# Halving each weighting of a strided-attention kernel, in a new order of the step

## The chip, the cores and the metric

One core of one Trainium2 chip runs the kernel. The metric is the device time of one execution in microseconds. Engines are named as in the profile: PE (TensorE) does matmuls, DVE (VectorE) and ACT (ScalarE) read their results, POOL (GpSimd) works in SBUF only, SP issues DMAs.

## The reference

`x` is 4 x 2048 x 256. After a layer norm, the result is `x` plus attention plus a linear layer whose input is rounded to fp8. The attention has 16 heads of 16 columns, and a key is allowed for a query when its number is a multiple of 4 ("far") or at most 8 away ("near"):

```python
allowed = (j % 4 == 0) | (jnp.abs(i - j) <= 8)
scores = jnp.einsum('bhqd,bhkd->bhqk', q, k) / jnp.sqrt(D)      # D = 16
attn = softmax(jnp.where(allowed, scores, -inf))
out = jnp.einsum('bhqk,bhkd->bhqd', attn, v)                     # then @ o_w + o_b
return x + out + ffn                                             # ffn: fp8-rounded xn @ w8.T + bias
```

## The kernel before

A first part (to about 240 us) projects q, k and v, writes them to DRAM with the keys sorted by stride, and computes the linear layer into `base`. The second part, `part_attend`, is what the change touches; a last part multiplies by `o_w` and adds, from about 1137 us.

**Steps.** The attention is cut into 64 steps, `Step` (line 639): one step is 512 queries of one batch for a group of 4 heads. All engines run the same unrolled list of steps, each its own function, and meet at semaphores. In a step TensorE computes 16 far scores (`("far", r, h)`: 128 of the 512 far keys, head h, 512 queries, L1065) and 4 near scores (`("near", h)`, a mask product L1069 and four products L1071), each into one of four PSUM banks `ps_s`. ACT takes the exponential of each into `probs` (L948, L953).

**Units.** The maxima that are subtracted are found by a second set of products, with queries on the partitions: 16 far units (`far_unit(tile, h)`, L1095) and 4 near units (`near_unit(half, two)`, two mask products L1103 and four products L1109), each into one of three banks `ps_u`. DVE takes the maximum of each (L1019, L1022). These run ahead of the scores: the units of index 0 to AHEAD - 1 in the list `MAXIMA` belong to the next step, the others to the one after it. At index AHEAD DVE combines the two kinds into `peak` (L1003); POOL makes the negated fp16 parts of it (L807 to L813, `negmax`), TensorE turns them (`("negmax",)`, L1061), ACT copies them and issues two DMAs into rows of `q_op` (L932), and the next step's first score waits for those.

**Weighing.** `weigh(st, d, r)` multiplies `probs` by v, in fp32, for the four heads side by side in four groups of 32 columns of the array; all five rounds (four far, one near) add up in one bank, `ps_o`. The last column group of v holds ones, which gives the sums. A weighing waits until ACT has written the probabilities of its round. `weigh_own` is of this step, `weigh_last` of the step before. After the last one ACT copies `ps_o` to `out_rows` (L917, at `COPY_AFTER`) and moves the sums by DMA (L924). DVE takes their reciprocal at index TURN (L996), SP stores it and loads it spread over rows (L868, L889), POOL multiplies (L800), SP stores the result (L894). Between these SP loads q (L87), k (L78, L79) and v (L831) of later steps in pieces.

**Order.** TensorE's order within a step is written out in `body` of `tensor_attend`: a score, a unit, a score, a unit, and a weighing after every few of these pairs. A score uses the upper or lower half of the array's rows by its head (heads 0 and 1, heads 2 and 3), a unit likewise, and most pairs take one of each. `SCORES` gives the scores' order to the other engines, `MAXIMA` that of the units. A score waits for ACT's reading of the score four before it, a unit for DVE's reading of the unit three before it.

Of the kernel before, what the change touches and what calls it, by code (L numbers as in the profile page):

```python
# [15 lines left out]
P = 128  # L16
KC = H // P
CH = 512
# [72 lines left out]
def part_project(nc, io, dram, keep, ctx):  # L91
# [526 lines left out]
COPY_AFTER, MOVE_AFTER = ("far", 1, 1), ("far", 1, 2)  # L618
LOAD_AFTER = SCORES[SCORES.index(("negmax",)) + 1]
MAXIMA = (  # L620
    ("far", 0, 2), ("far", 0, 3), ("far", 0, 0), ("far", 0, 1), ("near", 1, 0),
    ("far", 1, 2), ("near", 0, 0), ("far", 1, 0), ("far", 1, 3), ("far", 1, 1),
    ("far", 2, 2), ("far", 2, 3), ("far", 2, 0), ("far", 2, 1), ("near", 1, 1),
    ("far", 3, 2), ("far", 3, 0), ("far", 3, 3), ("near", 0, 1), ("far", 3, 1),
)


def entries(s):
# [5 lines left out]
def part_attend(nc, io, dram, keep, out, ctx, done):  # L634
# [146 lines left out]
    def gpsimd_attend(pool):  # L781

        pool.wait_ge(done["base_ready"], B * CPB)
        heads_k = k_op[1][:].rearrange("r (h s) -> r h s", h=PAIR)
        nc.gpsimd.memset(heads_k[:, :, NS:NS + WPAD], 0.0).then_inc(pads_set, 1)
        nc.gpsimd.memset(heads_k[:, :, WPAD + S:], 0.0).then_inc(pads_set, 1)
        nc.gpsimd.memset(share_rows[:], 1.0).then_inc(pads_set, 1)

        def add_bias(c):
            rows = base[:, c].rearrange("p (t f) -> p t f", t=TT)  # L790
            nc.gpsimd.tensor_tensor(rows, rows, keep["bias"][:].unsqueeze(1).broadcast_to([P, TT, H]),
                                    ALU.add).then_inc(bias_added, 1)
# [24 lines left out]
        unrolled(body)  # L817

    def sync_attend(sp):
# [86 lines left out]
            sp.dma_start(out_tiles[B * CPB - 1, :, t], totals[:, B * CPB - 1, t]).then_inc(out_stored, 16)  # L906
        sp.wait_ge(out_stored, 16 * (B * CPB - 1 + TT))

    def scalar_attend(act):

        def copy_out(st):
# [23 lines left out]
        def body(st):  # L935
            todo = st.entries()
            for kind in todo:
                act.wait_ge(s_ready, st.entry(kind))
                if kind[0] == "negmax":
                    if st.n >= 1:  # L940
                        act.wait_ge(negmax_loaded, 16 * HALVES * st.at())
                    ins = nc.scalar.activation(negmax_rows[:, st.n % 2],
                                               ps_s[st.bank(kind)][0:PARTS * HG * TT, 0:P], ACT.Copy)
                elif kind[0] == "far":
                    r, h = kind[1:]
                    if h == 0 and st.n >= 1:
                        act.wait_ge(pv_done, ROUNDS * st.at(-1) + r + 1)
                    ins = nc.scalar.activation(probs[:, r, h], ps_s[st.bank(kind)], ACT.Exp)  # L948
                else:
                    h = kind[1]  # L950
                    if h == 0 and st.n >= 1:
                        act.wait_ge(pv_done, ROUNDS * st.at())
# [94 lines left out]
    def tensor_attend(pe):  # L1047
# [66 lines left out]
        def weigh(st, d, r):  # L1114

            v = v_op[st.parity(d)]
            if r == 0:
# [4 lines left out]
            if r < ROUNDS - 1:  # L1122
                pe.wait_ge(s_used, st.entry(("far", r, HG - 1), d))
                for h in range(HG):
                    ins = nc.tensor.matmul(ps_o[h * VW:(h + 1) * VW], v[:, r, h * VW:(h + 1) * VW], probs[:, r, h],  # L1125
                                           start=(r == 0), stop=False)
            else:
                pe.wait_ge(s_used, st.entry(("near", HG - 1), d))
                for t in range(TT):
                    tile = NS // P + st.queries(d) * TT + t  # L1130
                    for h in range(HG):
                        ins = nc.tensor.matmul(ps_o[h * VW:(h + 1) * VW, t * P:(t + 1) * P],  # L1132
                                               v[0:WIN, tile, h * VW:(h + 1) * VW],
                                               probs[0:WIN, r, h, t * P:(t + 1) * P],
                                               start=False, stop=(t == TT - 1))
            ins.then_inc(pv_done, 1)

        def body(st):
            def far_unit(tile, h):
                unit(st, ("far", tile, h))  # L1140
# [4 lines left out]
            def far(r, h):  # L1145
                if st.exists():
                    score(st, ("far", r, h))

            def near(h):
                if st.exists():  # L1150
                    score(st, ("near", h))
# [2 lines left out]
                if ("negmax",) in st.entries():  # L1154
                    score(st, ("negmax",))

            def weigh_last(r):
                if st.exists(-1):
                    weigh(st, -1, r)

            def weigh_own(r):
                if st.exists():
                    weigh(st, 0, r)

            far(0, 0)
            far_unit(0, 2)
            far(0, 1)
            far_unit(0, 3)
            weigh_last(3)
            far(0, 2)  # L1170
            far_unit(0, 0)
            far(0, 3)
            far_unit(0, 1)
            far(1, 0)
            near_unit(1, 0)
            weigh_last(4)
            far(1, 1)
            far_unit(1, 2)
            far(1, 2)
            near_unit(0, 0)  # L1180
            far(1, 3)
            far_unit(1, 0)
            near(0)
            far_unit(1, 3)
            weigh_own(0)
            near(2)
            far_unit(1, 1)
            far(2, 0)
            far_unit(2, 2)
            far(2, 1)  # L1190
            far_unit(2, 3)
            far(2, 2)
            far_unit(2, 0)
            far(2, 3)
            far_unit(2, 1)
            weigh_own(1)
            maxima()
            far(3, 0)
            near_unit(1, 1)
            far(3, 1)  # L1200
            far_unit(3, 2)
            far(3, 2)
            far_unit(3, 0)
            near(1)
            far_unit(3, 3)
            weigh_own(2)
            near(3)
            near_unit(0, 1)
            far(3, 3)
            far_unit(3, 1)  # L1210

        def project(j, n):

# [153 lines left out]
```

## Time and profile before

| | |
|---|---|
| time, median of 3 runs | 1197.07 us (1196.61 to 1198.26) |
| profiled execution, its own time | 1197.61 us |
| its span, first to last instruction | 1195.8 us |
| busy: PE, DVE, ACT, POOL | 1114.0 (93%), 996.0 (83%), 803.0 (67%), 240.8 (20%) us |
| chain that ended last | PE 73%, DVE 16%, issue 5%, POOL 3%, ACT 2% |
| dearest groups, busy us | DVE L1019 652.9; ACT L948 554.6; PE L1095 326.2; PE L1065 308.6; PE L1125 274.5 |

The busy time of PE counts each matmul from its start to its modelled end, and consecutive matmuls overlap; so the distance between starts tells more than the length of one. In a timeline a line `x2` merges two instructions that follow each other; a bracket at its end is the time that the engine sat idle before it, and what released it.

### The profile page before, as it was taken

What the parts mean: (1) busy time and instruction counts of PE and PEld (TensorE: products, weight loads), DVE (VectorE), ACT (ScalarE), POOL (GpSimd) and SP (SyncE); (2) the same over time, 40 slices, a digit from 0 to 9 for tenths busy, and PEclk for the clock granted to TensorE, in tenths of its full rate; (3) what the DMA queues carried; (4) which work ended last, traced back from release to release, by engine and by line L of the source; (5) the groups of instructions that cost most, each with busy time, mean ns of one, the idle gap of its engine ahead of it and who ended that gap; (6) DMA issues with size and microseconds to landing.
All of it is one profiled execution on the core that took longest, in us unless ns stands there. A gap on an engine that the chain in (4) does not pass through costs nothing.

```text
span 1195.8 us, 27662 instructions
## 1 busy us (share of the span) xinstructions
PE 1114.0 (93%) x10178; PEld 562.5 (47%) x10178; DVE 996.0 (83%) x1842; ACT 803.0 (67%) x1528; POOL 240.8 (20%) x318
## 2 busy tenths in 40 slices
PE   5799999999999999999999999999999999999999
PEld 3466666634444444444444444444444444444387
DVE  6778887498999999998999999999999989999333
ACT  3343344327888888888888888888888788888800
POOL 2233333301121212212121212122121212122100
PEclk9899999959999999999999999999999999999999
DMA  4566667632222323223232223222322222232278
GB/s 156 163 189 185 193 201 196 204 95 53 67 69 71 82 64 81 62 78 74 71 75 68 69 72 78 72 76 62 76 76 71 75 68 70 74 78 57 60 255 273
DMA packets 184913, 124.44 MB, mean 104 GB/s; under 512 B 50824, under 2 KB 169352, under 8 KB 184776
## 3 DMA queue, kind: packets, MB, share of 16 engines
q1 hardware_dynamic: 169888, 114.81, 34.7%
q10 hardware_dynamic: 14896, 7.93, 2.5%
q8 instruction: 78, 1.28, 0.5%
q14 instruction: 51, 0.42, 0.1%
HBM read 70.61 MB, written 50.99 MB: 102 GB/s over the span
## 4 chain that ended last, share of the span: by engine, by line
PE 73%; DVE 16%; issue 5%; POOL 3%; ACT 2%; ACTq 0%; DMA 0%; DVEq 0%; POOLq 0%
PE ps_attend L1125 21%; PE ps_attend L1095 11%; PE ps_attend L1065 8%; DVE peak_far L1019 8%; PE ps_attend L1132 5%; PE ps_attend L1069 5%; PE ps_attend L1224 4%; DVE peak_near L1022 3%; PE ps_attend L1071 3%; PE ps_attend L1109 3%; PE ps_project L563 3%; PE ps_project L573 3%; PE ps_attend L1103 3%; POOL y L288 1%; PE ps_project L588 1%
## 5 line engine op out<-in xcount | busy, mean ns | idle before, releaser
L1019 DVE TENSOR_REDUCE peak_far<-ps_attend 128x1 f32<-128x512 f32 x1024 | 652.9, 679 | 44.3 <-PE ps_attend L1095 39.5
L948 ACT ACTIVATE probs<-ps_attend 128x512 f32<-128x512 f32 x1024 | 554.6, 601 | 119.3 <-PE ps_attend L1065 58.2
L1095 PE MATMUL ps_attend<-k_op,q_op 48*128 48x512 f16 x1024 | 326.2, 389 | 49.2 <-DVE peak_far L1019 45.6
L1065 PE MATMUL ps_attend<-q_op,k_op 50*128 50x512 f16 x1024 | 308.6, 382 | 0.8 <-ACT probs L953 0.4
L1125 PE MATMUL ps_attend<-probs,v_op 128*32 128x512 f32 x2048 | 274.5, 608 | 2.8 <-ACT probs L948 2.1
L1022 DVE TENSOR_REDUCE peak_near<-ps_attend 128x4 f32<-128x432 f32 x256 | 154.0, 602 | 34.1 <-PE ps_attend L1109 34.1
L807 POOL TENSOR_SCALAR peak_rest<-peak 128x16 f32<-128x16 f32 x64 | 16.1, 252 | 704.7 <-DVE peak L1003 704.7
L1095 PEld LDWEIGHTS ps_attend<-k_op,q_op 48*128 48x128 f16 x1024 | 84.8, 94 | 140.5 <-DVE peak_far L1019 97.3
L953 ACT ACTIVATE probs<-ps_attend 108x512 f32<-108x512 f32 x256 | 144.8, 597 | 3.5 <-PE ps_attend L1071 3.3
L1065 PEld LDWEIGHTS ps_attend<-q_op,k_op 50*128 50x128 f16 x1024 | 86.2, 94 | 125.4 <-ACT probs L948 82.8
L1103 PE MATMUL ps_attend<-mask_k,mask_q 48*128 48x216 bf16 x512 | 116.7, 259 | 0.4 <-DVE peak_far L1019 0.4
L1109 PE MATMUL ps_attend<-k_op,q_op 48*128 48x108 f16 x1024 | 115.2, 209 | 0.0
L1071 PEld LDWEIGHTS ps_attend<-q_op,k_op 50*108 50x108 f16 x1024 | 93.3, 125 | 35.4 <-issue 1.1
L1069 PE MATMUL ps_attend<-mask_q,mask_k 48*108 48x512 bf16 x256 | 102.4, 400 | 0.0
L1109 PEld LDWEIGHTS ps_attend<-k_op,q_op 48*128 48x128 f16 x1024 | 96.7, 95 | 8.1
L1071 PE MATMUL ps_attend<-q_op,k_op 50*108 50x128 f16 x1024 | 99.1, 216 | 0.0
L800 POOL TENSOR_TENSOR out_rows<-out_rows,share_rows 128x512 f32<-128x512 f32 x64 | 82.0, 1281 | 31.1 <-DMA share_rows<-shares_dram 28.0
L1069 PEld LDWEIGHTS ps_attend<-mask_q,mask_k 48*108 48x108 bf16 x256 | 31.7, 124 | 109.0 <-ACT probs L948 104.8
L1125 PEld LDWEIGHTS ps_attend<-probs,v_op 128*32 128x32 f32 x2048 | 40.8, 108 | 63.0 <-issue 32.1
L1132 PE MATMUL ps_attend<-probs,v_op 108*32 108x128 f32 x2048 | 69.1, 276 | 0.0
L285 POOL TENSOR_TENSOR quant<-quant,power 128x1024 f32<-128x1024 f32 x16 | 38.5, 2404 | 125.9 <-PE ps_project L588 99.6
L537 PE MATMUL ps_project<-xnT,wq 128*128 128x512 f32 x128 | 59.3, 607 | 2.1 <-DVE wq L395 2.1
(87 smaller groups left out, 1017.2 us busy)
## 6 DMA issues: line engine op xcount, KB each, us to landing
v_dram<-v_sb SPq DMA_DIRECT2D x64, 256.0 KB, 3.0
v_op<-v_dram SPq DMA_DIRECT2D x48, 288.0 KB
q_op<-q_parts_dram SPq DMA_DIRECT2D x384, 32.0 KB, 1.9
k_op<-k_parts_dram SPq DMA_DIRECT2D x96, 96.0 KB, 2.6
base<-in_x SPq DMA_DIRECT2D x16, 512.0 KB, 4.9
q_parts_dram<-qk_parts SPq DMA_DIRECT2D x32, 256.0 KB, 3.0
share_rows<-shares_dram SPq DMA_DIRECT2D x256, 32.0 KB, 2.3
attn_dram<-out_rows SPq DMA_DIRECT2D x256, 32.0 KB, 1.7
```

The costliest lines, as they stand in the source:

```text
L948: ins = nc.scalar.activation(probs[:, r, h], ps_s[st.bank(kind)], ACT.Exp)
L953: ins = nc.scalar.activation(probs[0:WIN, ROUNDS - 1, h], ps_s[st.bank(kind)][0:WIN], ACT.Exp)
L1019: ins = nc.vector.tensor_reduce(peak_far[:, h, tile:tile + 1], bank, AX_X, ALU.max)
L1022: ins = nc.vector.tensor_reduce(peak_near[:, half * PAIR:(half + 1) * PAIR, two * 2:two * 2 + 2], near_bank(bank), AX_X, ALU.max)
L1065: ins = nc.tensor.matmul(bank, k[rows, keys(h, r * P, P)], q[rows, h % PAIR], start=True, stop=True)
L1069: nc.tensor.matmul(bank[0:WIN], mask_k[masks], mask_q[masks, at:at + CH], start=True, stop=False)
L1071: ins = nc.tensor.matmul(bank[0:WIN, t * P:(t + 1) * P], k[rows, window(h, st.queries() * TT + t)], q[rows, h % PAIR, t * P:(t + 1) * P], ...
L1095: ins = nc.tensor.matmul(bank, q[rows, h % PAIR, tile * P:(tile + 1) * P], k[rows, keys(h, 0, NS)], start=True, stop=True)
L1103: nc.tensor.matmul(near_bank(bank)[:, :, t], mask_q[masks, at + tile * P:at + (tile + 1) * P], mask_k[masks].unsqueeze(1).broadcast_to([MA ...
L1109: ins = nc.tensor.matmul(near_bank(bank)[:, r, t], q[rows, r, tile * P:(tile + 1) * P], k[rows, window(h, st.queries(d) * TT + tile)], sta ...
L1125: ins = nc.tensor.matmul(ps_o[h * VW:(h + 1) * VW], v[:, r, h * VW:(h + 1) * VW], probs[:, r, h], start=(r == 0), stop=False)
L1132: ins = nc.tensor.matmul(ps_o[h * VW:(h + 1) * VW, t * P:(t + 1) * P], v[0:WIN, tile, h * VW:(h + 1) * VW], probs[0:WIN, r, h, t * P:(t + ...
```

## The change

Each weighing is made in `SPLIT` = 2 parts. A part of a far round takes 256 of the 512 queries (columns) for the four heads; a part of the near round takes two of the four tiles. The semaphore `pv_done` counts after the second part, in the order of the new list `WEIGHINGS`: far 0, far 1, far 2, near, far 3 (`weighed` gives ACT its values). Only the first part of far 0 starts the accumulation.

The order of the step is new: after every second pair of score and unit stands one part. The four near scores and the four near units stand together, pairs 13 to 16. The last three parts of a step (near 1, far 3 0 and 1) stand behind pairs 2, 4 and 6 of the next. AHEAD goes from 10 to 4, so `peak` is made after four units of the list, and the units of tile 3 lead it; the `negmax` product follows pair 10 and not pair 14. TURN goes from 17 to 14. On POOL the multiplication of `out_rows` moves from ahead of the `negmax` chain to behind it, with its wait one step later.

```diff
-AHEAD = 10
-TURN = 17
+AHEAD = 4
+TURN = 14
 SCORES = (
     ("far", 0, 0), ("far", 0, 1), ("far", 0, 2), ("far", 0, 3), ("far", 1, 0),
-    ("far", 1, 1), ("far", 1, 2), ("far", 1, 3), ("near", 0), ("near", 2),
-    ("far", 2, 0), ("far", 2, 1), ("far", 2, 2), ("far", 2, 3), ("negmax",),
-    ("far", 3, 0), ("far", 3, 1), ("far", 3, 2), ("near", 1), ("near", 3),
+    ("far", 1, 1), ("far", 1, 2), ("far", 1, 3), ("far", 2, 0), ("far", 2, 1),
+    ("negmax",), ("far", 2, 2), ("far", 2, 3), ("near", 0), ("near", 1),
+    ("near", 2), ("near", 3), ("far", 3, 0), ("far", 3, 1), ("far", 3, 2),
     ("far", 3, 3),
 )
...
+WEIGHINGS = (("far", 0), ("far", 1), ("far", 2), ("near",), ("far", 3))
+SPLIT = 2
...
         def body(st):
-            if st.exists(-3):
-
-                rows = out_rows[:, (st.n - 3) % OUTS]
-                pool.wait_ge(negmax_ready, min(st.at(1), STEPS))
-                pool.wait_ge(shares_loaded, 16 * HG * st.at(-2))
-                nc.gpsimd.tensor_tensor(rows, rows, share_rows[:], ALU.mult).then_inc(attn_ready, 1)
             if st.exists(1):
 
-                if st.exists(-3):
-                    pool.wait_ge(attn_ready, st.at(-2))
                 pool.wait_ge(peak_ready, st.at(2))
...
+            if st.exists(-3):
+
+                rows = out_rows[:, (st.n - 3) % OUTS]
+                pool.wait_ge(negmax_ready, min(st.at(2), STEPS))
+                pool.wait_ge(shares_loaded, 16 * HG * st.at(-2))
+                nc.gpsimd.tensor_tensor(rows, rows, share_rows[:], ALU.mult).then_inc(attn_ready, 1)
...
+        def weigh(st, d, kind, part):
+
+            v, n = v_op[st.parity(d)], CH // SPLIT
+            cols = slice(part * n, (part + 1) * n)
...
                 for h in range(HG):
-                    ins = nc.tensor.matmul(ps_o[h * VW:(h + 1) * VW], v[:, r, h * VW:(h + 1) * VW], probs[:, r, h],
-                                           start=(r == 0), stop=False)
+                    ins = nc.tensor.matmul(ps_o[h * VW:(h + 1) * VW, cols], v[:, r, h * VW:(h + 1) * VW],
+                                           probs[:, r, h, cols], start=(kind == WEIGHINGS[0] and part == 0),
+                                           stop=(kind == WEIGHINGS[-1] and part == SPLIT - 1))
             else:
                 pe.wait_ge(s_used, st.entry(("near", HG - 1), d))
-                for t in range(TT):
+                for t in range(part * TT // SPLIT, (part + 1) * TT // SPLIT):
...
+            if part == SPLIT - 1:
+                ins.then_inc(pv_done, 1)
```

The order of a step after the change (it takes the place of the one in `body` above; `W` stands for `weigh_last` in the first three and `weigh_own` in the others):

```
far(0,0) far_unit(3,2)  far(0,1) far_unit(3,3)  W near 1
far(0,2) far_unit(3,0)  far(0,3) far_unit(3,1)  W far 3, 0
far(1,0) far_unit(0,2)  far(1,1) far_unit(0,3)  W far 3, 1
far(1,2) far_unit(0,0)  far(1,3) far_unit(0,1)  W far 0, 0
far(2,0) far_unit(1,2)  far(2,1) far_unit(1,3)  negmax  W far 0, 1
far(2,2) far_unit(1,0)  far(2,3) far_unit(1,1)  W far 1, 0
near(0) near_unit(1,0)  near(1) near_unit(1,1)  W far 1, 1
near(2) near_unit(0,0)  near(3) near_unit(0,1)  W far 2, 0
far(3,0) far_unit(2,2)  far(3,1) far_unit(2,3)  W far 2, 1
far(3,2) far_unit(2,0)  far(3,3) far_unit(2,1)  W near 0
```

## Rows read from the trace of the kernel before

**Rows 1.** Stretches: us; busy PE, PEld, DVE, ACT, POOL (instructions); clock; DMA; GB/s

```profile
400.00:1000.00 600.00, 565.27 (x6187) 254.73 (x6184) 545.48 (x965) 488.28 (x965) 110.78 (x187) 1.00 0.29 73
```

**Rows 2.** Timeline of VectorE, 607 to 625 us: start, length, engine, line, tiles, count, idle

```profile
607.09 0.69 DVE L1019 TENSOR_REDUCE peak_far<-ps_attend 128x1 f32<-128x512 f32 x1 [0.17 <-PE ps_attend L1095]
...
609.91 0.69 DVE L1019 TENSOR_REDUCE peak_far<-ps_attend 128x1 f32<-128x512 f32 x1 [0.42 <-PE ps_attend L1095]
...
610.84 2.48 DVE L1019 TENSOR_REDUCE peak_far<-ps_attend 128x1 f32<-128x512 f32 x4
...
615.25 0.24 DVE L996 RECIPROCAL shares<-sums 128x16 f32<-128x16 f32 x1
...
616.36 0.61 DVE L1022 TENSOR_REDUCE peak_near<-ps_attend 128x4 f32<-128x432 f32 x1 [0.32 <-PE ps_attend L1109]
616.88 3.20 DVE L1019 TENSOR_REDUCE peak_far<-ps_attend 128x1 f32<-128x512 f32 x5
...
624.51 2.48 DVE L1019 TENSOR_REDUCE peak_far<-ps_attend 128x1 f32<-128x512 f32 x4
```

**Rows 3.** Timeline of TensorE's matmuls, 603 to 617 us, same columns

```profile
603.35 0.39 PE L1095 MATMUL ps_attend<-k_op,q_op 48*128 48x512 f16 x1
603.67 1.06 PE L1125 MATMUL ps_attend<-probs,v_op 128*32 128x512 f32 x8
604.67 0.39 PE L1065 MATMUL ps_attend<-q_op,k_op 50*128 50x512 f16 x1
...
604.89 0.38 PE L1065 MATMUL ps_attend<-q_op,k_op 50*128 50x512 f16 x1
...
605.15 0.26 PE L1103 MATMUL ps_attend<-mask_k,mask_q 48*128 48x216 bf16 x1
...
605.62 1.08 PE L1132 MATMUL ps_attend<-probs,v_op 108*32 108x128 f32 x32
...
606.64 0.39 PE L1095 MATMUL ps_attend<-k_op,q_op 48*128 48x512 f16 x1
...
611.59 0.39 PE L1095 MATMUL ps_attend<-k_op,q_op 48*128 48x512 f16 x1 [0.54 <-DVE peak_far L1019]
...
615.51 0.42 PE L1069 MATMUL ps_attend<-mask_q,mask_k 48*108 48x512 bf16 x1
...
615.77 0.26 PE L1103 MATMUL ps_attend<-mask_k,mask_q 48*128 48x216 bf16 x1
...
615.99 0.38 PE L1065 MATMUL ps_attend<-q_op,k_op 50*128 50x512 f16 x1
...
616.16 0.42 PE L1095 MATMUL ps_attend<-k_op,q_op 48*128 48x512 f16 x2
```

**Rows 4.** Timeline of ACT and its DMA queue (ACTq), 613 to 616 us, same columns

```profile
613.37 1.29 ACTq L932 DMA_DIRECT2D q_op<-negmax_rows  x2
614.71 1.08 ACT L948 ACTIVATE probs<-ps_attend 128x512 f32<-128x512 f32 x2 [0.75 <-PE ps_attend L1071]
```

**Rows 5.** Groups by shape, 400 to 1000 us: count; busy us, mean ns; idle before

```profile
L1125 PE MATMUL ps_attend<-probs,v_op 128*32 128x512 f32 x1400 | 186.4, 604 | 0.8 <-ACT probs L948 0.6
...
L1132 PE MATMUL ps_attend<-probs,v_op 108*32 108x128 f32 x1408 | 47.6, 276 | 0.0
...
L1125 PEld LDWEIGHTS ps_attend<-probs,v_op 128*32 128x32 f32 x1400 | 27.9, 108 | 42.2 <-issue 22.8 <-ACT probs L948 10.7 <-ACT out_rows L917 8.7
```

**Rows 6.** DMA issues by line, 400 to 1000 us: count, KB each, median us to landing

```profile
k_op<-k_parts_dram SPq DMA_DIRECT2D x66, 96.0 KB, 2.6
```

**Rows 7.** Line 1003 (`peak`): ns min/median/max, first and last start in us

```profile
L1003 DVE TENSOR_TENSOR peak<-peak_far,peak_near x64: 174/174/176, 252.3 to 1117.1; 128x16 f32<-128x16 f32 x64
```

**Rows 8.** Timeline of VectorE, the third `peak`

```profile
282.04 0.17 DVE L1003 TENSOR_TENSOR peak<-peak_far,peak_near 128x16 f32<-128x16 f32 x1
```

**Rows 9.** The page's slices of 29.9 us each, granted TensorE clock in tenths

```profile
PEclk9899999959999999999999999999999999999999
```

**Rows 10.** Timeline of ACT, the last exponential

```profile
1134.05 0.59 ACT L948 ACTIVATE probs<-ps_attend 128x512 f32<-128x512 f32 x1
```

More of the change, by code:

```diff
@@ L620 @@
 MAXIMA = (
[L621 to L624, printed above, removed]
-)
+    ("far", 3, 2), ("far", 3, 3), ("far", 3, 0), ("far", 3, 1), ("far", 0, 2),
+    ("far", 0, 3), ("far", 0, 0), ("far", 0, 1), ("far", 1, 2), ("far", 1, 3),
+    ("far", 1, 0), ("far", 1, 1), ("near", 1, 0), ("near", 1, 1), ("near", 0, 0),
+    ("near", 0, 1), ("far", 2, 2), ("far", 2, 3), ("far", 2, 0), ("far", 2, 1),
+)
+WEIGHINGS = (("far", 0), ("far", 1), ("far", 2), ("near",), ("far", 3))
+SPLIT = 2
 def entries(s):
@@ L907, in sync_attend, with weighed @@
         sp.wait_ge(out_stored, 16 * (B * CPB - 1 + TT))
+    def weighed(st, kind):
+        return ROUNDS * st.at(-1) + WEIGHINGS.index(kind) + 1
     def scalar_attend(act):
@@ L946, in body @@
                     if h == 0 and st.n >= 1:
-                        act.wait_ge(pv_done, ROUNDS * st.at(-1) + r + 1)
+                        act.wait_ge(pv_done, weighed(st, ("far", r)))
                     ins = nc.scalar.activation(probs[:, r, h], ps_s[st.bank(kind)], ACT.Exp)
@@ L951, in body @@
                     if h == 0 and st.n >= 1:
-                        act.wait_ge(pv_done, ROUNDS * st.at())
+                        act.wait_ge(pv_done, weighed(st, ("near",)))
                     ins = nc.scalar.activation(probs[0:WIN, ROUNDS - 1, h], ps_s[st.bank(kind)][0:WIN], ACT.Exp)
@@ L1112, in unit @@
             ins.then_inc(u_ready, 1)
-        def weigh(st, d, r):
-            v = v_op[st.parity(d)]
-            if r == 0:
+        def weigh(st, d, kind, part):
+            v, n = v_op[st.parity(d)], CH // SPLIT
+            cols = slice(part * n, (part + 1) * n)
+            if kind == WEIGHINGS[0] and part == 0:
                 if st.queries(d) == 0:
@@ L1121, in weigh @@
                     pe.wait_ge(out_copied, st.at(d))
-            if r < ROUNDS - 1:
+            if kind[0] == "far":
+                r = kind[1]
                 pe.wait_ge(s_used, st.entry(("far", r, HG - 1), d))
                 for h in range(HG):
-                    ins = nc.tensor.matmul(ps_o[h * VW:(h + 1) * VW], v[:, r, h * VW:(h + 1) * VW], probs[:, r, h],
-                                           start=(r == 0), stop=False)
+                    ins = nc.tensor.matmul(ps_o[h * VW:(h + 1) * VW, cols], v[:, r, h * VW:(h + 1) * VW],
+                                           probs[:, r, h, cols], start=(kind == WEIGHINGS[0] and part == 0),
+                                           stop=(kind == WEIGHINGS[-1] and part == SPLIT - 1))
             else:
                 pe.wait_ge(s_used, st.entry(("near", HG - 1), d))
-                for t in range(TT):
+                for t in range(part * TT // SPLIT, (part + 1) * TT // SPLIT):
                     tile = NS // P + st.queries(d) * TT + t
@@ L1133, in weigh @@
                                                v[0:WIN, tile, h * VW:(h + 1) * VW],
-                                               probs[0:WIN, r, h, t * P:(t + 1) * P],
-                                               start=False, stop=(t == TT - 1))
-            ins.then_inc(pv_done, 1)
+                                               probs[0:WIN, ROUNDS - 1, h, t * P:(t + 1) * P],
+                                               start=False, stop=False)
+            if part == SPLIT - 1:
+                ins.then_inc(pv_done, 1)
         def body(st):
@@ L1155, in maxima, with weigh_last, weigh_own @@
                     score(st, ("negmax",))
-            def weigh_last(r):
+            def weigh_last(kind, part):
                 if st.exists(-1):
-                    weigh(st, -1, r)
-            def weigh_own(r):
+                    weigh(st, -1, kind, part)
+            def weigh_own(kind, part):
                 if st.exists():
-                    weigh(st, 0, r)
+                    weigh(st, 0, kind, part)
             far(0, 0)
+            far_unit(3, 2)
+            far(0, 1)
+            far_unit(3, 3)
@@ L1166, in body @@
+            weigh_last(("near",), 1)
+            far(0, 2)
+            far_unit(3, 0)
+            far(0, 3)
+            far_unit(3, 1)
+            weigh_last(("far", 3), 0)
+            far(1, 0)
             far_unit(0, 2)
-            far(0, 1)
+            far(1, 1)
             far_unit(0, 3)
-            weigh_last(3)
-            far(0, 2)
+            weigh_last(("far", 3), 1)
+            far(1, 2)
             far_unit(0, 0)
-            far(0, 3)
+            far(1, 3)
             far_unit(0, 1)
-            far(1, 0)
+            weigh_own(("far", 0), 0)
@@ L1175, in body @@
+            far(2, 0)
+            far_unit(1, 2)
+            far(2, 1)
+            far_unit(1, 3)
+            maxima()
+            weigh_own(("far", 0), 1)
+            far(2, 2)
+            far_unit(1, 0)
+            far(2, 3)
+            far_unit(1, 1)
+            weigh_own(("far", 1), 0)
+            near(0)
             near_unit(1, 0)
[L1176 to L1179, printed above, removed]
+            near(1)
+            near_unit(1, 1)
@@ L1180, in body @@
+            weigh_own(("far", 1), 1)
+            near(2)
             near_unit(0, 0)
[L1181 to L1206, printed above, removed]
             near(3)
             near_unit(0, 1)
+            weigh_own(("far", 2), 0)
+            far(3, 0)
+            far_unit(2, 2)
+            far(3, 1)
+            far_unit(2, 3)
+            weigh_own(("far", 2), 1)
+            far(3, 2)
+            far_unit(2, 0)
@@ L1209, in body @@
             far(3, 3)
-            far_unit(3, 1)
+            far_unit(2, 1)
+            weigh_own(("near",), 0)
         def project(j, n):
```

## The prediction

> **What bounds the kernel now.** I read the page's chain first: TensorE holds 73% of it and VectorE 16%, almost all in the attention part. A row of stretches gives the steady part: in 600 us TensorE's matmuls are busy 565 us and VectorE 545 us, ACT 488, at the full granted clock [rows 1]. Two engines above 90% and neither at 100% is a coupled loop; its period is read from the order of events, so the rest rests on the timeline of one step. VectorE takes 20 maxima per step (16 "far", 4 "near"). Running without a wait it starts a far maximum every 0.624 us (five in 3.20, less the last one's own 0.70, is four intervals) and the next one 0.52 us after a near one (616.36 to 616.88). The combining operation `peak` stretches one interval to 0.93 (609.91 to 610.84), 0.31 more; the reciprocal (615.25) adds 0.12 beside its neighbours [rows 2]. Without waits a step is 16 x 0.624 + 4 x 0.517 + 0.31 + 0.12 = 12.5 us; it takes 13.67 (610.84 to 624.51), and the difference is four waits, of which the first, second and last stand in the rows (607.09, 609.91, 616.36: idle 0.17, 0.42 and 0.32). Each is for a unit, the product whose maximum is taken, that TensorE made late, and before each TensorE had done a whole weighing (that before 607.09 at 605.62) [rows 2, 3]. ACT is the third engine: some 11.1 us of a step busy and about 0.8 held by its own DMA issues (idle before 614.71) [rows 1, 4].
>
> **Prices on TensorE.** A far score and a far unit use different halves of the rows and run together, 0.22 us for a pair (604.67 to 604.89). From a far unit to the weighing behind it 0.32 pass (603.35 to 603.67), 0.10 more than a pair; from the weighing to the next pair 1.00 (604.67) [rows 3]. One of its fp32 instructions of 512 columns lasts 604 ns, one of 128 columns 276 ns: 384 columns are 328 ns, 512 are 0.43 us [rows 5]. Two such passes stream 0.86, and 0.14 is the change back. So a weighing is 0.10 + 0.86 + 0.14, and the 0.24 doesn't shrink with its columns. The near weighing, in four times as many instructions of a quarter of the columns, takes 1.02 (605.62 to 606.64): more weight loads and shorter instructions cost 0.02 in all [rows 3].
>
> **Part by part.** *Halving.* Ten parts in place of five weighings. A part is 0.10 + 0.43 + 0.14 = 0.67, of which 0.565 from its start to the next pair. Five added parts are 5 x 0.24 = 1.2 us of TensorE per step; the 32 added instructions of a step's far weighings and their weight loads hide as in the near one. Bounds for an added part: not below 0.14 (the change back alone), up to 0.35, if one load of 0.108 stood open in each [rows 5]. I take 0.24.
>
> The Trainium skill (TensorEngine Tiling, Key Properties) says that changing the tiling mode, not only the tile, drains the engine. The 0.10 and the 0.14 at a weighing's two ends agree with that; the page has no price, and by its rule the change adds ten drains per step and is a loss wherever TensorE ends last.
>
> *Where the parts hide.* Three banks hold units. A bank is free 0.75 after the start of the maximum read from it (610.84 to the unit at 611.59); a unit can be read 0.45 after its start (606.64, maximum 607.09) [rows 2, 3]. In far stretches TensorE needs 0.22 + 0.32 + 0.565 = 1.11 for two pairs and a part, VectorE 1.25. Set the start of a maximum to 0: the unit into its bank starts at 0.75, the part at 1.07, the next pair at 1.63, its unit is readable at 2.08, and VectorE wants it at 2.50. So in 16 of 20 pairs there is no wait. With a whole weighing it is readable at 2.52, just late, and anything slow behind it is a wait: the four of before.
>
> *The near stretch.* The new order puts four near scores beside four near units in a row. The trace has one such pair per step: score 615.51, unit 615.77, next score 615.99, next unit 616.16, and the near unit is read at 616.36 [rows 2, 3]. So: 0.48 to the next score; the unit 0.26 behind its score after a weighing (0.22 otherwise, the score's mask product); readable 0.59 after its start; and 0.47 from a near unit to the weighing behind it (605.15 to 605.62). Walk on, 0 being the maximum of pair 9. Unit of pair 12 at 0.75 (its bank), part 1.07. Pair 13 at 1.63, readable 2.48; pair 14 at 2.11, unit 2.33, readable 2.92; part 2.80. Pair 15 at 3.37, unit 3.63, readable 4.22; pair 16 at 3.85, unit 4.07, readable 4.66; part 4.54. Pair 17, far, at 5.10, readable 5.55. VectorE: pairs 9 to 12 at 0, 0.62, 1.25, 1.87; 13 at 2.50; 14 at 3.01; 15 at 4.22 (wanted 3.53); 16 at 4.73; 17 at 5.55 (wanted 5.25). Without waits pair 17 would start at 4.57, so the near stretch costs 0.98. The reciprocal now stands before pair 15, in the first wait: its 0.12 is hidden. Pairs 19 and 21 are readable at 6.66 and 7.77, wanted at 6.80 and 8.05: no wait. **Period: 12.05 + 0.31 + 0.98 = 13.35**, 0.31 less than now. Three parts lie on this path: if a part costs d more, the period is 3d longer.
>
> *The moved steps.* `peak` comes after unit 4 and the negmax product after pair 10, six pairs (3.7 us) between them and not four: no wait. ACT's two DMA issues follow pair 11; the first score that needs a bank behind them (four ahead) has about 0.9 us in hand. The copy-out now waits for the part behind pair 6, 0.1 us on ACT, and two pairs later TensorE asks for it with some 0.3 in hand. POOL's multiplication moves behind the negmax chain of the step; SP waits for it ahead of four share loads, four stores and its last K or V pieces, so it issues them some 2 us later in the step than now, the last K piece about 11.5 us in. That lands 2.6 us later (median) [rows 6] and pair 5 of the next step asks for it, at 13.35 + 2.8: 2 us of cover, one step in four. All taken at nothing; with the K cover gone and 1 us more it would be 16 us.
>
> *Both ends.* The steps from the third `peak` to the last (282.04 to 1117.1) are 61: 61 x 0.31 = **-18.9** [rows 7, 8]. With the limit at 4, sixteen units and not ten stand alone before the first scores: first to second `peak` 20 x 0.62 + 0.2 = 12.6. TensorE's clock is at the lower of its levels, 1.2 GHz, in this part of the span (the ninth slice of 30 us at 0.5 in the granted row) [rows 9], so up to about 275 us streaming doubles: pairs 5 to 8 3.7, 9 to 12 4.0, 13 and 14 3.0, then at the upper level 1.8, 2.5, 2.5 and 0.3 for `peak`, 17.8 to the third. Together 30.4 against the 29.7 from 252.3 to 282.04: **+0.7**. At the end 36 pairs and not 30 run without units; the 30 took 1117.1 to 1134.65, the end of the last exponential, 0.59 each: **+3.5**. Behind that exponential stand two far parts, not a far and a near weighing: 1.2 and not 2.0, **-0.8** [rows 10]. Sum -15.5, from the profiled execution's own 1197.6 (span 1195.8) to 1182.1; that execution is 0.5 above the median of 1197.1, so **1181.6 us**.
>
> **Rivals.** (A) *An added part is cheaper*, or near pairs pack closer. For: some of the 0.24 may belong to the neighbours. At 0.14 it is 3 x 0.10 x 61 = 18 us less: 1163. The floor, no waits at all, is 61 x 1.2 = 73 less: near 1127. (B) *Slower: near pairs in a row don't overlap.* The one near pair of the trace is followed by a far one. If a near score waits until the near unit before it is through (616.16 and not 615.99), 0.17 comes on the path in each of the two groups: 0.34 x 61 = 21, **1202**. It decides against the change from 15.5 / 61 = 0.25 per step, 0.13 per group. Against: the score at 615.99 did start while the near unit ran. (C) *A weight load of 0.108 stands open in each part*: 3 x 0.108 x 61 = 20, 1201. Against: the near weighing. (D) *The change doesn't do what it says*, the wait only moves: ACT held by copy-out and issues, or SP's late K piece, eats the 0.25: 1197.
>
> **How the numbers follow.** Forecast (1172 to 1191) 0.50; A 0.13; B 0.13; C 0.10; D 0.14. Faster by over 0.2% (about what a measurement here can tell from no change) takes the forecast, A and a third of D: 0.68; same the larger part of the rest of D, 0.09; slower B and C: 0.23. The range reaches A's price and those of B and C: 1160 to 1204.
>
> **What would show it.** `peak` to `peak` 13.35. In VectorE's timeline two waits, before the third near maximum (0.6) and the first far one behind the near ones (0.3), none between far ones, the reciprocal free. On TensorE 0.565 from a part to the next score; 4096 instructions of 256 columns near 0.39 us each. Near score to near score 0.48 is right, 0.65 is B. A part above 0.65 to the next score is C. A unit waiting for K once in four steps, or scores waiting for ACT in each, is D. Most wrong of all would be waits between far pairs.

## The result and the profile after

The changed kernel takes 1163.5 us (median of 4 runs, 1163.0 to 1168.9) against 1196.9 us of the kernel before on the same chip: a ratio of 0.973, 95% interval 0.970 to 0.976. That is 33.4 us less. The forecast was 15.5 us less, 1181.6. The measured time lies below the 1172 to 1191 of the forecast itself and inside the whole range (1160 to 1204) only because that reaches down to the price of rival A.

The page's chain of the changed kernel, by engine:

```profile
PE 85%; DVE 6%; issue 4%; POOL 3%; ACT 1%; DVEq 0%; POOLq 0%
```

TensorE's share rises from 73% to 85%, VectorE's falls from 16% to 6%. The stretch that answers to [rows 1] (busy PE, weight loads, DVE, ACT, POOL; clock; DMA):

```profile
400.00:1000.00 600.00, 597.89 (x7929) 250.75 (x7930) 563.47 (x1006) 518.91 (x1007) 113.16 (x191) 1.00 0.30 76
```

More work fits into the same 600 us: 1006 instructions on VectorE and not 965, at the same clock. The timeline of VectorE, one step, answers to [rows 2] (L1023 and L1026 are the far and the near maxima, L1007 is `peak`):

```profile
606.47 0.18 DVE L1007 TENSOR_TENSOR peak<-peak_far,peak_near 128x16 f32<-128x16 f32 x1
606.68 4.87 DVE L1023 TENSOR_REDUCE peak_far<-ps_attend 128x1 f32<-128x512 f32 x8
611.55 1.12 DVE L1026 TENSOR_REDUCE peak_near<-ps_attend 128x4 f32<-128x432 f32 x2
612.59 0.24 DVE L1000 RECIPROCAL shares<-sums 128x16 f32<-128x16 f32 x1
613.31 1.12 DVE L1026 TENSOR_REDUCE peak_near<-ps_attend 128x4 f32<-128x432 f32 x2 [0.47 <-PE ps_attend L1113]
614.68 4.87 DVE L1023 TENSOR_REDUCE peak_far<-ps_attend 128x1 f32<-128x512 f32 x8 [0.25 <-PE ps_attend L1099]
619.58 0.17 DVE L1007 TENSOR_TENSOR peak<-peak_far,peak_near 128x16 f32<-128x16 f32 x1
```

`peak` to `peak` is 13.11 us. There are two marked waits, where the forecast had them: before the third near maximum and before the first far one behind the near ones. The eight far maxima in a row have no wait between them, and they need 4.87 us less the last one's 0.69: seven intervals of 0.60. That is the number to look at.

TensorE's matmuls in the same kernel answer to [rows 3]: two far pairs with a part behind them, then the near pairs.

```profile
603.33 0.39 PE L1099 MATMUL ps_attend<-k_op,q_op 48*128 48x512 f16 x1
603.55 0.38 PE L1069 MATMUL ps_attend<-q_op,k_op 50*128 50x512 f16 x1
603.55 0.38 PE L1099 MATMUL ps_attend<-k_op,q_op 48*128 48x512 f16 x1
603.86 0.65 PE L1139 MATMUL ps_attend<-probs,v_op 108*32 108x128 f32 x16
604.44 0.39 PE L1069 MATMUL ps_attend<-q_op,k_op 50*128 50x512 f16 x1
...
610.13 0.64 PE L1131 MATMUL ps_attend<-probs,v_op 128*32 128x256 f32 x8
610.70 0.42 PE L1073 MATMUL ps_attend<-mask_q,mask_k 48*108 48x512 bf16 x1
...
611.18 0.38 PE L1073 MATMUL ps_attend<-mask_q,mask_k 48*108 48x512 bf16 x1
```

(L1099 are the far units, L1069 the far scores, L1073 the first product of a near score, L1131 and L1139 the far and the near parts.) A part begins 0.31 after the last unit (603.55 to 603.86), and the next score 0.57 or 0.58 after the part (610.13 to 610.70, 603.86 to 604.44). Near score to near score is 0.48 (610.70 to 611.18). So every price on TensorE came out as taken, within 0.02 us.

### The profile page after: what moved, and what is told of

It is laid out like the page before. It is cut to its first block, busy times and chain, and to the rows that moved or that the text cites. A ratio compares the mean times of both kernels' runs of the same rounds, so it can differ in the third digit from the quotient of the medians.

```text
span 1161.2 us, 31698 instructions
## 1 busy us (share of the span) xinstructions
PE 1127.3 (97%) x12226; PEld 541.6 (47%) x12226; DVE 988.1 (85%) x1842; ACT 816.5 (70%) x1528; POOL 241.5 (21%) x318
## 4 chain that ended last, share of the span: by engine, by line
PE 85%; DVE 6%; issue 4%; POOL 3%; ACT 1%; DVEq 0%; POOLq 0%
PE ps_attend L1131 24%; PE ps_attend L1069 23%; PE ps_attend L1139 6%; PE ps_attend L1237 4%; PE ps_attend L1073 4%; PE ps_attend L1099 4%; PE ps_attend L1113 4%; PE ps_attend L1107 3%; PE ps_project L563 3%; PE ps_project L573 3%; PE ps_attend L1075 3%; DVE peak_far L1023 2%; POOL y L288 1%; PE ps_project L588 1%; DVE xn L446 1%
## 5 line engine op out<-in xcount | busy, mean ns | idle before, releaser
L1023 DVE TENSOR_REDUCE peak_far<-ps_attend 128x1 f32<-128x512 f32 x1024 | 623.8, 680 | 18.9 <-PE ps_attend L1099 16.5
L952 ACT ACTIVATE probs<-ps_attend 128x512 f32<-128x512 f32 x1024 | 563.9, 596 | 102.7 <-PE ps_attend L1069 30.9
L1099 PE MATMUL ps_attend<-k_op,q_op 48*128 48x512 f16 x1024 | 345.3, 392 | 5.7 <-DVE peak_far L1023 2.9
L1131 PE MATMUL ps_attend<-probs,v_op 128*32 128x256 f32 x4096 | 328.9, 392 | 0.7 <-ACT out_rows L921 0.7
L1069 PE MATMUL ps_attend<-q_op,k_op 50*128 50x512 f16 x1024 | 311.0, 384 | 0.0
L1026 DVE TENSOR_REDUCE peak_near<-ps_attend 128x4 f32<-128x432 f32 x256 | 143.7, 602 | 30.5 <-PE ps_attend L1113 30.3
L957 ACT ACTIVATE probs<-ps_attend 108x512 f32<-108x512 f32 x256 | 138.3, 595 | 14.7 <-PE ps_attend L1075 14.7
L1069 PEld LDWEIGHTS ps_attend<-q_op,k_op 50*128 50x128 f16 x1024 | 57.0, 94 | 183.1 <-ACT probs L952 142.6
L1099 PEld LDWEIGHTS ps_attend<-k_op,q_op 48*128 48x128 f16 x1024 | 90.0, 93 | 98.0 <-DVE peak_far L1023 90.4
L1131 PEld LDWEIGHTS ps_attend<-probs,v_op 128*32 128x32 f32 x4096 | 81.6, 108 | 99.5 <-issue 31.6
L1073 PE MATMUL ps_attend<-mask_q,mask_k 48*108 48x512 bf16 x256 | 101.9, 398 | 0.0
L813 POOL TENSOR_TENSOR out_rows<-out_rows,share_rows 128x512 f32<-128x512 f32 x64 | 81.7, 1277 | 35.2 <-DMA share_rows<-shares_dram 30.4
L1139 PE MATMUL ps_attend<-probs,v_op 108*32 108x128 f32 x2048 | 82.3, 279 | 0.0
L1139 PEld LDWEIGHTS ps_attend<-probs,v_op 108*32 108x32 f32 x2048 | 48.2, 109 | 39.2 <-ACT probs L952 39.2
```

The lines of the kernel that those rows point to most:

```text
L1023: ins = nc.vector.tensor_reduce(peak_far[:, h, tile:tile + 1], bank, AX_X, ALU.max)
L1026: ins = nc.vector.tensor_reduce(peak_near[:, half * PAIR:(half + 1) * PAIR, two * 2:two * 2 + 2], near_bank(bank), AX_X, ALU.max)
L1069: ins = nc.tensor.matmul(bank, k[rows, keys(h, r * P, P)], q[rows, h % PAIR], start=True, stop=True)
L1073: nc.tensor.matmul(bank[0:WIN], mask_k[masks], mask_q[masks, at:at + CH], start=True, stop=False)
L1099: ins = nc.tensor.matmul(bank, q[rows, h % PAIR, tile * P:(tile + 1) * P], k[rows, keys(h, 0, NS)], start=True, stop=True)
L1131: ins = nc.tensor.matmul(ps_o[h * VW:(h + 1) * VW, cols], v[:, r, h * VW:(h + 1) * VW], probs[:, r, h, cols], start=(kind == WEIGHINGS[0] ...
```

## The experiments

The runs ask two things: how much of the gain is the halving and how much the order, and whether the forecast missed by VectorE's pace or by the price of a part. `peak` to `peak` is the common measure: 13.66 in the kernel before (610.63 to 624.30 makes 13.67), 13.11 in the changed one.

**Whole weighings in the new order.**

```diff
-SPLIT = 2
+SPLIT = 1
...
-            weigh_last(("far", 3), 0)
...
-            weigh_last(("far", 3), 1)
+            weigh_last(("far", 3), 0)
```

(and likewise for the others: near behind pair 2, far 0 behind 10, far 1 behind 14, far 2 behind 18.)

> The changed kernel with SPLIT = 1: five whole weighings, behind pairs 2, 6, 10, 14 and 18 of the new order. Theory N (the new order brings most of the gain, the halving little): walking the step with 0.60 us per far maximum, peak to peak is 13.26 us against 13.11 of the changed kernel (one wait of 0.8 before the third near maximum, 0.1 to 0.2 behind each weighing in far stretches), so about 1173 us. Theory H (halving brings the gain, since a whole weighing is too long for three banks): back near the 13.66 of the kernel before, 1197 us.

Measured: 1175.2 us, ratio 0.982 (0.980 to 0.985), and from `peak` to `peak` in VectorE's timeline 13.32:

```profile
613.16 0.18 DVE L1007 TENSOR_TENSOR peak<-peak_far,peak_near 128x16 f32<-128x16 f32 x1
613.37 5.03 DVE L1023 TENSOR_REDUCE peak_far<-ps_attend 128x1 f32<-128x512 f32 x8
618.32 1.11 DVE L1026 TENSOR_REDUCE peak_near<-ps_attend 128x4 f32<-128x432 f32 x2
...
620.18 1.12 DVE L1026 TENSOR_REDUCE peak_near<-ps_attend 128x4 f32<-128x432 f32 x2 [0.59 <-PE ps_attend L1113]
621.22 5.22 DVE L1023 TENSOR_REDUCE peak_far<-ps_attend 128x1 f32<-128x512 f32 x8
626.48 0.17 DVE L1007 TENSOR_TENSOR peak<-peak_far,peak_near 128x16 f32<-128x16 f32 x1
```

Eight far maxima in 5.03 or 5.22 and not 4.87: the waits behind whole weighings (0.16 and 0.35) carry no bracket. The new order without the halving brings 22 of the 33 us, the halving in that order the other 12. Theory N holds. "Order" here takes in all that the change moves: AHEAD, TURN and POOL's multiplication. Only TURN was run by itself (below), so how the 22 us divide among the rest isn't shown.

**Halves in the old order.**

```diff
             far_unit(0, 3)
-            weigh_last(3)
+            weigh_last(3, 0)
             far(0, 2)
             far_unit(0, 0)
+            weigh_last(3, 1)
```

(each of the five so, the second half one pair later.)

> The kernel before, in its old order, with each weighing halved and the second half one pair later. Theory N: the halving takes away part of each wait and gives it back in five more changes of tiling on a TensorE that has little to spare: peak to peak 13.5, give or take 0.2, about 1188 us. Theory H: the halves bring the whole gain, 13.1, 1163 us.

Measured: 1200.7 us (seven executions, 1197.0 to 1205.9), ratio 1.004 (1.003 to 1.006); `peak` to `peak` 13.69 in the profiled execution, the fastest of them (609.15 to 622.84). The halving alone brings nothing. My 1188 was too low by 1%: that order puts halves beside near units in three places, and I had not walked it through. In its timeline the three marked waits of a step stand at a near maximum or at the far one right behind it (0.18 before 612.57, 0.31 before 615.44, 0.33 before 620.27). What decides between the theories, that it isn't 1163, is clear.

**Whole weighings away from the near pairs.**

```diff
-COPY_AFTER, MOVE_AFTER = ("far", 1, 1), ("far", 1, 2)
+COPY_AFTER, MOVE_AFTER = ("far", 1, 0), ("far", 1, 1)
...
-SPLIT = 2
+SPLIT = 1
```

(near behind pair 2, far 3 behind 5, far 0 behind 8, far 1 behind 11, far 2 behind 18.)

> SPLIT = 1, whole weighings behind pairs 2, 5, 8, 11 and 18, so that none stands among the four near pairs or right ahead of them; the copy-out one exponential earlier. Theory N, that what a weighing costs depends on what stands behind it: each far weighing makes VectorE wait 0.12, the near stretch nothing: peak to peak 12.67, about 1136 us. Theory H: whole weighings cost as in the kernel before, 13.6 or more, 1195 us.

Measured: 1142.1 us, ratio 0.954 (0.952 to 0.956), 21 us faster than the change with five parts fewer:

```profile
612.62 0.17 DVE L1007 TENSOR_TENSOR peak<-peak_far,peak_near 128x16 f32<-128x16 f32 x1
612.83 5.23 DVE L1023 TENSOR_REDUCE peak_far<-ps_attend 128x1 f32<-128x512 f32 x8
617.97 1.11 DVE L1026 TENSOR_REDUCE peak_near<-ps_attend 128x4 f32<-128x432 f32 x2
619.00 0.24 DVE L1000 RECIPROCAL shares<-sums 128x16 f32<-128x16 f32 x1
619.16 1.05 DVE L1026 TENSOR_REDUCE peak_near<-ps_attend 128x4 f32<-128x432 f32 x2
620.13 5.23 DVE L1023 TENSOR_REDUCE peak_far<-ps_attend 128x1 f32<-128x512 f32 x8
625.40 0.18 DVE L1007 TENSOR_TENSOR peak<-peak_far,peak_near 128x16 f32<-128x16 f32 x1
```

That is 12.78, and 12.67 was forecast. The near maxima follow each other without a wait, and this step of 20 maxima has no bracket at all, yet it is 0.67 longer than the 12.11 without waits. By the rows it is the two groups of eight, at 5.23 and not 4.87, some 0.35 each.

**The near pairs cleared, halves elsewhere.**

```diff
             weigh_own(("far", 1), 0)
+            weigh_own(("far", 1), 1)
...
-            weigh_own(("far", 1), 1)
...
-            weigh_own(("far", 2), 0)
...
+            weigh_own(("far", 2), 0)
             weigh_own(("far", 2), 1)
```

> The changed kernel with the two parts among the near pairs taken out of them: far 1 whole behind pair 12, far 2 whole behind pair 18, all else as it is. The walk gives no wait between near maxima any more, but 0.52 before the first (a whole weighing right ahead of it) and 0.2 behind pair 18: 12.11 + 0.72 = 12.85, about 1148 us. If the near pairs themselves, and not the parts among them, were what VectorE waits for, no gain: 1163.

Measured: 1143.1 us, ratio 0.955 (0.954 to 0.957), `peak` to `peak` 12.80 (610.35 to 623.15); the forecasts were 1148 us and 12.85:

```profile
610.35 0.17 DVE L1007 TENSOR_TENSOR peak<-peak_far,peak_near 128x16 f32<-128x16 f32 x1
610.55 4.87 DVE L1023 TENSOR_REDUCE peak_far<-ps_attend 128x1 f32<-128x512 f32 x8
615.86 1.12 DVE L1026 TENSOR_REDUCE peak_near<-ps_attend 128x4 f32<-128x432 f32 x2 [0.43 <-PE ps_attend L1113]
616.90 0.24 DVE L1000 RECIPROCAL shares<-sums 128x16 f32<-128x16 f32 x1
617.06 1.05 DVE L1026 TENSOR_REDUCE peak_near<-ps_attend 128x4 f32<-128x432 f32 x2
618.03 5.08 DVE L1023 TENSOR_REDUCE peak_far<-ps_attend 128x1 f32<-128x512 f32 x8
623.15 0.17 DVE L1007 TENSOR_TENSOR peak<-peak_far,peak_near 128x16 f32<-128x16 f32 x1
```

The wait between the near maxima is gone and the one before them is there, 0.51 from start to start beyond the pace (610.55 + 8 x 0.60 = 615.35, measured 615.86) where the walk had 0.52. What cost in the near stretch was the parts, not the pairs.

**The reciprocal moved.**

```diff
-TURN = 14
+TURN = 18
```

> The changed kernel with TURN at 18 and not 14: the reciprocal stands between two far maxima, where VectorE has no wait, and not in the wait before the third near maximum. If its 0.12 us were hidden there, as the prediction had it, each step gets 0.12 longer, 7 us, about 1171 us. If the wait before the third near maximum isn't what ends last there, or TensorE's lead swallows it, no change: 1163.5.

Measured: 1170.0 us, ratio 0.978 (0.976 to 0.979), 6.5 us above the changed kernel; 13.22 from `peak` to `peak` (601.75 to 614.97). The wait before the third near maximum grows from 0.47 to 0.64, and the reciprocal now stands between two far maxima (611.16). So the 0.12 was hidden where the prediction had it.

**Twice the instructions in the same places.**

```diff
-SPLIT = 2
+SPLIT = 4
...
             weigh_own(("far", 0), 0)
+            weigh_own(("far", 0), 1)
```

(two quarters wherever a half stood, with twice the instructions in the far parts.)

> SPLIT = 4, but always two quarters in one place, where the changed kernel has one half: the same ten places and changes of tiling, twice the instructions and weight loads, 128 columns each. If only changes of tiling cost, a part lasts as long as now (0.57 to the next score), peak to peak 13.1, 1164 us. If weight loads stand open at short matmuls (rival C), three parts on the path with 0.1 each give 13.4, 1182 us. Of the clock: if it stayed at its lower level in e4_quarter for the short instructions, it stays there here too and the time goes beyond 1500 us; if for the twenty changes and pairs, it rises here as in the changed kernel.

Measured: 1164.5 us, ratio 0.973 (0.971 to 0.975), within 0.1% of the changed kernel, at the full clock. By shape, in 400 to 1000 us (count, busy us, mean ns, idle before):

```profile
L1131 PE MATMUL ps_attend<-probs,v_op 128*32 128x128 f32 x5844 | 236.0, 278 | 0.0
```

So 5844 matmuls in a stretch, and not the 2924 of the changed kernel, cost nothing. Rival C is refuted: twice the weight loads add no time. The 0.24 of a part is in the changes at its ends, as the trace's 0.31 and 0.57 say. This agrees with the drain at a change of tiling mode of the Trainium skill (TensorEngine Tiling, Key Properties).

**Quarters behind every pair.**

```diff
-SPLIT = 2
+SPLIT = 4
...
             far_unit(0, 2)
+            weigh_last(("far", 3), 2)
             far(1, 1)
             far_unit(0, 3)
-            weigh_last(("far", 3), 1)
+            weigh_last(("far", 3), 3)
```

> SPLIT = 4: twenty parts of 128 queries, one behind each pair. Theory N (each part costs 0.24 us of TensorE that doesn't shrink with its columns): a far pair with its part takes 0.32 + 0.35 = 0.67, a near one 1.08, a step 16 x 0.67 + 4 x 1.08 = 15.1 us, TensorE never waiting; about 1285 us. Rival A of the prediction (an added part costs 0.14 or less): a far pair with its part 0.57, under VectorE's 0.60, a step 12.9, 1150 us.

Measured: 1977.6 us, ratio 1.65, half as long again as forecast. The stretch and two pairs of TensorE's timeline:

```profile
400.00:1000.00 600.00, 595.70 (x5501) 217.50 (x5495) 319.81 (x510) 291.46 (x509) 56.12 (x97) 0.50 0.16 39
```

```profile
803.97 0.61 PE L1099 MATMUL ps_attend<-k_op,q_op 48*128 48x512 f16 x1
804.51 0.66 PE L1131 MATMUL ps_attend<-probs,v_op 128*32 128x128 f32 x8
805.10 0.60 PE L1069 MATMUL ps_attend<-q_op,k_op 50*128 50x512 f16 x1
```

The granted clock is 0.50, the lower level of 1.2 GHz, through the whole attention part: it fell while units stood alone (0.50 from 245 us on, as in the kernels before and after) and never rose, where theirs rose between 268 and 272 us. The run before this one has the same short instructions and its clock rose, so they alone don't hold it down. The 15.1 us at the upper level weren't tested; no run shows them. What the rows do show is the price of the changes at the lower level: 0.54 from unit to part, where a pair takes 0.40 to 0.43 at that level (265.95 to 266.35 and 259.68 to 260.11 in the changed kernel), and 0.59 from part to score, where streaming takes an estimated 0.44 (two instructions of 128 columns, 0.11 each by [rows 5], doubled for the clock). Together that is 0.26 to 0.29, against 0.24 at the upper level: it hardly depends on the clock, and at neither level is it the 0.14 of rival A.

**Almost no columns.** Only far 0 is whole, and it multiplies the identity in place of the probabilities; the other parts take 32 columns of 256.

```diff
-            cols = slice(part * n, (part + 1) * n)
+            cols = slice(part * n, (part + 1) * n if kind == WEIGHINGS[0] else part * n + 32)
...
+                        src = keep["ident"][:].unsqueeze(1).broadcast_to([P, 2, P])
```

> The changed kernel with nearly all columns of the weighings left out: only far 0 is whole (on the identity in place of the probabilities), every other part takes 32 columns of 256. The changes of tiling stay, the streaming goes. What VectorE does without waits is then seen. Theory P (my 0.624 us per far maximum held an unmarked wait, the true pace is 0.60): far maxima 0.60 apart everywhere, peak to peak 12.11, about 1102 us. Theory Q (0.624 is the pace and the parts were cheaper than forecast): 12.5, about 1126 us.

Measured: 1205.4 us, ratio 1.007 (1.005 to 1.010): not faster than the kernel before, though most of the weighing is left out. TensorE's granted clock in the 600 us from 400 on is 0.80 on average, again and again at its lower level. A step that meets it (0.59 on average from 622.5 to 629 us) waits among its far maxima:

```profile
400.00:1000.00 600.00, 585.25 (x6906) 240.34 (x6905) 544.13 (x969) 479.28 (x969) 110.90 (x187) 0.80 0.29 73
```

```profile
617.60 4.87 DVE L1023 TENSOR_REDUCE peak_far<-ps_attend 128x1 f32<-128x512 f32 x8
622.50 0.17 DVE L1007 TENSOR_TENSOR peak<-peak_far,peak_near 128x16 f32<-128x16 f32 x1
622.71 2.48 DVE L1023 TENSOR_REDUCE peak_far<-ps_attend 128x1 f32<-128x512 f32 x4
625.68 1.29 DVE L1023 TENSOR_REDUCE peak_far<-ps_attend 128x1 f32<-128x512 f32 x2 [0.49 <-PE ps_attend L1099]
```

As a floor for the whole kernel it failed, and its time says nothing on P or Q. Where VectorE doesn't wait, the pace is 0.60 here too (4.87 for eight, 2.48 for four), which is P.

**A version that beats both.**

```diff
-COPY_AFTER, MOVE_AFTER = ("far", 1, 1), ("far", 1, 2)
+COPY_AFTER, MOVE_AFTER = ("far", 0, 3), ("far", 1, 0)
...
             far_unit(3, 3)
+            weigh_last(("near",), 0)
             weigh_last(("near",), 1)
...
             far_unit(3, 1)
             weigh_last(("far", 3), 0)
+            weigh_last(("far", 3), 1)
...
             far_unit(0, 0)
+            weigh_own(("far", 0), 0)
+            weigh_own(("far", 0), 1)
```

(so near is whole behind pair 2, far 3 behind 4 and far 0 behind 7; far 1 is halved behind pairs 10 and 12, far 2 behind 18 and 20.)

> No part among the near pairs. Near whole behind pair 2, far 3 whole behind pair 4 and far 0 whole behind pair 7 (there the peak gives VectorE 0.31 more of its own), far 1 halved behind pairs 10 and 12, far 2 halved behind 18 and 20; copy-out two exponentials earlier. Theory N: a whole weighing costs VectorE 0.12 in a far stretch and nothing beside the peak, a half nothing, a half right ahead of the near pairs 0.08: peak to peak 12.11 + 0.12 + 0.08 + 0.1 left over as in e2_free = 12.4, about 1119 us. Rival: ACT, with 11.5 us of work and DMA issues per step, takes over as the bound, 12.7 or more, 1138 us.

Measured: 1126.3 us, ratio 0.941 (0.940 to 0.943): 37 us below the changed kernel, 71 below the one before. `peak` to `peak` is 12.53:

```profile
603.75 0.18 DVE L1007 TENSOR_TENSOR peak<-peak_far,peak_near 128x16 f32<-128x16 f32 x1
604.03 4.87 DVE L1023 TENSOR_REDUCE peak_far<-ps_attend 128x1 f32<-128x512 f32 x8
609.07 1.12 DVE L1026 TENSOR_REDUCE peak_near<-ps_attend 128x4 f32<-128x432 f32 x2 [0.16 <-PE ps_attend L1113]
...
610.27 1.05 DVE L1026 TENSOR_REDUCE peak_near<-ps_attend 128x4 f32<-128x432 f32 x2
611.24 5.01 DVE L1023 TENSOR_REDUCE peak_far<-ps_attend 128x1 f32<-128x512 f32 x8
616.28 0.17 DVE L1007 TENSOR_TENSOR peak<-peak_far,peak_near 128x16 f32<-128x16 f32 x1
```

Before the near maxima stand 0.24 of wait (0.16 in the bracket) where the walk had 0.08, and 0.14 among the far ones where it had 0.12. Behind `peak`, where a whole weighing was to cost nothing, the next far maximum starts 0.28 after it and not 0.21. In all that is some 0.1 more per step than was taken, 1126 us and not 1119. ACT has 519 us busy in 600 here, as in the changed kernel, so it hasn't become the bound.

## Why the prediction was off

The sign, the mechanism and the places of the waits were right; the forecast was half of the gain that came. The step that failed is the first number of the first part: "running without a wait it starts a far maximum every 0.624 us". That was a mean of four intervals in one row of [rows 2], taken for a run without waits because it has no bracket. Asked for smaller windows, the same row of the kernel before comes apart (each line is two maxima, start of the first and length of both):

```profile
617.48 1.28 DVE L1019 TENSOR_REDUCE peak_far<-ps_attend 128x1 f32<-128x512 f32 x2
...
618.08 1.41 DVE L1019 TENSOR_REDUCE peak_far<-ps_attend 128x1 f32<-128x512 f32 x2
618.79 1.29 DVE L1019 TENSOR_REDUCE peak_far<-ps_attend 128x1 f32<-128x512 f32 x2
```

Starts are at 616.88, 617.48, 618.08 and 618.79: 0.60, 0.60 and 0.71. The third interval is a wait for the unit that TensorE makes behind a whole weighing. The weighing and the next unit in its timeline:

```profile
617.34 1.06 PE L1125 MATMUL ps_attend<-probs,v_op 128*32 128x512 f32 x8
...
618.34 0.39 PE L1095 MATMUL ps_attend<-k_op,q_op 48*128 48x512 f16 x1
```

The unit starts at 618.34 and is readable 0.45 later, 618.79. A maximum lasts 0.68 and the next one starts 0.60 after it, overlapping it by 0.08. So a start that comes late by less than 0.08 leaves no idle time, and one late by 0.11 only 0.03, which the merged timeline swallows. The same row `x4 2.48` of [rows 2] gives (2.48 - 0.69) / 3 = 0.60, and I had not compared the two.

The closing of the sum hid it. 12.5 and 1.11 of brackets (0.17, 0.42, 0.20 and 0.32) are 13.6, near the 13.67 measured. With the true pace a step without waits is 9.6 + 2.07 + 0.31 + 0.12 = 12.1, and the brackets understate: each counts from the end of the maximum before, 0.08 late, so four hide 0.3, and the unmarked wait 0.11 more. The two mistakes, about 0.4 each, were opposite.

- **Period.** The walk through the near stretch stands: it has pair 17 at 5.55 after pair 9, the rows have 5.60 (609.08 to 614.68). The other intervals are 4 x 0.60 and 7 x 0.60 + 0.91, together 13.11, as measured. The forecast had 13.35, nearly all of the difference from 0.624 in these eleven intervals and not 0.60. That is 0.24 in each of 61 steps, 14.6 us. The steps from the third to the last `peak` went from 835.1 to 800.1 us (278.66 to 1078.8), 34.9 less and not 18.9; the other 1.4 us are from the steps' means, 13.69 and 13.12 and not 13.66 and 13.11.
- **Prices of a part** (0.32 and 0.565), of a near pair (0.48), the hidden reciprocal (0.12): right, by the rows of after and by the runs with TURN at 18 and with quarters in place. Rival A's time was met by luck: its cause, a cheaper part or closer near pairs, is refuted. So are B (0.48 in the rows) and C.
- **Far stretches without a wait:** right, 4.87 for eight. They gain more than I took, since what was "just late" there in the kernel before was already a wait on 0.60.
- **Head.** First to third `peak` 27.4 us (251.2 to 278.66) and not 30.4, so 3 us were taken too many. TensorE's clock rose earlier than the 275 us taken: it was 0.62 on average from 268 to 270 us and 1.00 from then on (in the kernel before 0.51 from 270 to 272 us), though the first far score began later (259.68 us, before 257.63).
- **Tail.** Last `peak` to the end of the last exponential 22.1 us (to 1100.93) against 17.6: +4.5, forecast +3.5. From there to the first product with `o_w` 1.9 and not 2.8: -0.9, forecast -0.8. All that isn't in the 61 steps came to +0.3, forecast +3.4; in that the first part counts -1.4, as VectorE's first far maximum starts at 239.23 us and not 240.59, in a part that the change doesn't touch. So the profiled executions differ by 34.6 us, 19.1 more than forecast: 14.6 by the pace, 1.4 by the means, 3.1 by the ends.
- **Moved steps.** SP waits for POOL's multiplication now; in the kernel before it waited for DVE's reciprocal (118.3 us in 44 times). Its queue, waits in 400 to 1000 us (us in total, times, longest):

```profile
SPq L889 <- POOL out_rows L813: 72.2, 45, 2.4
```

1.6 us in each step, and no unit waits for K and no part for V: cover as taken. D didn't come.

What stays open: why the halves in the old order lose the 0.2 us per step that I gave them, step by step; what AHEAD and the grouping of the near pairs bring each by itself; and the time of twenty parts at the upper clock.

## What to carry to other kernels

Take the pace of an engine from starts, in a stretch that nothing else feeds late, and compare two such stretches; a row without a bracket can hold waits, since a bracket counts only from the end of the instruction before, and here each overlaps the next by 0.08 us. When two sizes are inferred from one sum, that the sum closes proves neither.

An interruption of fixed length on the producer costs by what stands behind it: put it where the consumer's next items are slow to consume and quick to produce. Here whole weighings in the right places (1142 us) beat halves in the wrong ones (1163), and both together gave 1126.

## What the runs showed of the hardware

TensorE's granted clock didn't follow the busy share of its records. With twenty parts of 128 columns per step, one behind each pair, it stayed at 1.2 GHz, with 595.7 of 600 us busy. With eight of the ten parts thin it fell again and again (0.80 on average, 585 of 600 us busy). With 128-column matmuls in the ten places of the changed kernel it stood at 2.4 GHz. No run separates what it is about the twenty places that holds it down. The Trainium skill (TensorE: Matmul & The Clock Gate, HAM oscillation) puts a fall down to idle gaps between bursts of matmuls. In the records of the run with twenty parts the idle time is 4.3 of 600 us in all, so such gaps are not seen there and, as far as records tell, the two differ; whether the array stands still under the records, at the ends of a part, they don't show. With less work on TensorE, the kernel with thin parts was 42 us slower than the changed one.

Matmuls of different halves of the rows don't always start in program order. In the kernel before, the far score of 615.99 [rows 3] stands behind the near unit in the program and starts before that unit's last two products:

```profile
616.07 0.25 PE L1109 MATMUL ps_attend<-k_op,q_op 48*128 48x108 f16 x2
```

The near pairs of the changed kernel do the same: the second near score starts at 611.18, the last two products of the near unit before it at 611.26. So a near pair takes 0.48, and not the 0.65 of rival B.
